# Conv-attention and transformer block on one core: q product in natural order, first attention's matrix work reordered, second-matmul weight splits two steps later

## The reference

```python
# 1. convolutional attention, 1x1 convolutions, softmax along one image axis
q, k, v = (einsum('bchw,oc->bohw', x, w) + b for w, b in ...)   # q, k: 16 channels; v: 128
energy = einsum('bci,bcj->bij', q, k).reshape(b, h, w, h, w)
attn = softmax(energy, axis=-1)
x = gamma * einsum('bchk,bhwkv->bcwv', v, attn) + x
# 2. attention over the 256 tokens of each image, 8 heads of 16, softmax over the n axis
t = tokens(x);  y = layernorm(t)
k, q, v = y @ Wk, y @ Wq, y @ Wv
attn = softmax(einsum('bnhd,bmhd->bnmh', k, q) / 4, axis=n)
t = t + einsum('bnmh,bmhd->bnhd', attn, v)
# 3. mixture of 8 experts, the best 2 per token weighted, 128 -> 512 -> 128
y = layernorm(t);  logits = y @ gate.T;  comb = softmax over the top 2, else 0
for e in range(8):
    out += comb[:, e] * (gelu(y @ w1[e].T + b1[e]) @ w2[e].T + b2[e])
x = t + out
```

## Time and profile before

| | us |
|---|---|
| median of 3 runs | 186.25 (186.21 to 189.31) |
| the profiled execution | 186.13 |
| its span in the trace | 184.2 |
| PE busy | 174.1 (95%) |
| ACT busy | 123.2 (67%) |
| DVE busy | 117.1 (64%) |
| POOL busy | 79.5 (43%) |

### The profile page before, as it was taken

One profiled execution on the slowest core, in us unless ns is written; L12 is line 12 of the kernel. 1 busy time (PEld: TensorE's weight loads), 2 busy tenths in 40 slices (PEclk: granted clock), 3 DMA queues, 4 the chain that ended last, 5 costly groups with the idle time before them and its releaser, 6 DMA issues.

```text
span 184.2 us, 3336 instructions
## 1 busy us (share of the span) xinstructions
PE 174.1 (95%) x1277; PEld 118.6 (64%) x1277; DVE 117.1 (64%) x199; ACT 123.2 (67%) x185; POOL 79.5 (43%) x68
## 2 busy tenths in 40 slices
PE   6999999989898998999999999999999999999991
PEld 3267867665466544447466567567887888888880
DVE  1569544985465396456084959397888677676673
ACT  3516953317727743545988598867878999999970
POOL 8404228988703284452536093524151152333312
PEclk9999999999999999999999999999999999999999
DMA  5799200000000000570000000000000880000001
GB/s 141 276 374 419 96 0 0 4 0 4 0 5 0 2 0 4 181 271 7 0 0 5 0 0 0 4 0 0 0 7 4 244 269 0 0 4 0 0 0 57
DMA packets 5791, 10.94 MB, mean 59 GB/s; under 512 B 1280, under 2 KB 1664, under 8 KB 5520
## 3 DMA queue, kind: packets, MB, share of 16 engines
q1 hardware_dynamic: 5360, 10.65, 16.7%
q10 hardware_dynamic: 416, 0.08, 0.3%
HBM read 10.17 MB, written 0.56 MB: 58 GB/s over the span
## 4 chain that ended last, share of the span: by engine, by line
PE 73%; issue 8%; ACT 7%; POOL 4%; DVE 4%; DMA 2%; ACTq 0%; DVEq 0%; POOLq 0%
PE PS L1159 9%; PE PS L1163 7%; PE PS L1160 7%; PE PS L1186 6%; PE PS L1189 6%; PE PS L1187 6%; PE PS L1181 4%; POOL pairs L357 4%; PE PS L1017 3%; PE PS L1031 3%; ACT room L516 2%; PE PS L910 2%; PE PS L878 2%; PE PS L1104 2%; DMA convw_sb<-convw 2%
## 5 line engine op out<-in xcount | busy, mean ns | idle before, releaser
L516 ACT ACTIVATE room<-PS,b_sb 128x512 f32<-128x512 f32 x64 | 43.6, 688 | 22.6 <-PE PS L1163 21.2
L772 DVE TENSOR_TENSOR Gl<-room,Gh 128x512 fp32r<-128x512 f32 x50 | 41.2, 831 | 13.7 <-ACT Gh L461 13.0
L365 POOL TENSOR_TENSOR x_sb<-x_sb,room 128x512 f32<-128x512 f32 x15 | 23.6, 1572 | 56.0 <-DVE room L781 56.0
L1159 PE MATMUL PS<-x2h,w1h 128*128 128x512 f32 x64 | 27.4, 427 | 1.2 <-ACT room L516 0.8
L461 ACT ACTIVATE Gh<-room 128x512 fp32r<-128x512 f32 x40 | 25.3, 633 | 1.3
L1163 PE MATMUL PS<-x2l,w1h 128*128 128x512 f32 x64 | 25.5, 398 | 0.0
L1160 PE MATMUL PS<-x2h,w1l 128*128 128x512 f32 x64 | 25.2, 393 | 0.0
L1186 PE MATMUL PS<-Gh,w2h 128*128 128x512 f32 x50 | 20.8, 416 | 0.0
L1187 PE MATMUL PS<-Gh,w2l 128*128 128x512 f32 x50 | 19.8, 395 | 0.0
L1189 PE MATMUL PS<-Gl,w2h 128*128 128x512 f32 x50 | 19.7, 395 | 0.0
L1159 PEld LDWEIGHTS PS<-x2h,w1h 128*128 128x128 f32 x64 | 12.0, 187 | 10.6 <-issue 4.9
(11 more groups left out here) (136 smaller groups left out, 294.2 us busy)
## 6 DMA issues: line engine op xcount, KB each, us to landing
room<-comb_rows SPq DMA_DIRECT2D x16, 256.0 KB, 5.2
w1raw<-w SPq DMA_DIRECT2D x8, 256.0 KB, 5.9
w_sb<-w SPq DMA_DIRECT2D x2, 1024.0 KB, 10.6
x_sb<-x SPq DMA_DIRECT2D x2, 256.0 KB, 3.2
dev<-xk SPq DMA_DIRECT2D x1, 512.0 KB, 6.3
out<-x_sb SPq DMA_DIRECT2D x2, 256.0 KB, 4.2
attw_sb<-attw SPq DMA_DIRECT2D x1, 320.0 KB, 6.8
cst<-consts SPq DMA_DIRECT2D x1, 228.5 KB, 6.5
```

The costliest lines, as they stand in the source:

```text
L365: nc.gpsimd.tensor_tensor(t2[:, cols(p)], t2[:, cols(p)], part[:, s, :], ALU.add).then_inc(acc_done, 1)
L516: nc.scalar.activation(G[:, n % GR, :], PS[:, U_BANK[n % 2], :], ACT.Gelu, bias=b1_sb[:, c:c + 1])\
L772: nc.vector.tensor_tensor(Gl[:, n % GR, :], G[:, n % GR, :], Gh[:, n % GR, :].bitcast(f32), ALU.subtract)\
L1159: mm(o, w1h[e][:, ms], x2h[:, cols(p)], start=True, stop=False)
```

## The change

Three edits. The q product of the conv stage takes x in its natural order, and the two copies read PSUM by columns instead. In the first attention the third `project_second` moves ahead of the second raw run, V's projection behind the third raw run and the transposes (whose bank changes from 0 to 1, with the waits adjusted), and `scores(3, s)` stand ahead of `sums(0)` and `sums(1)`. `LOW_W2` shifts `low_weights2` by two steps in POOL's list.

```diff
+        def by_columns(images):
+            return images.rearrange("c (b h w) -> c b w h", b=2, h=H)
...
-        NMT_BANK = [((0, 0), (0, TOK)), ((2, 0), (3, 0))]
+        NMT_BANK = [((1, 0), (1, TOK)), ((2, 0), (3, 0))]
...
-        LOW_W2 = {n + 1: e for n, e in enumerate(W2_ORDER)}
+        LOW_W2 = {n + 3: e for n, e in enumerate(W2_ORDER)}
...
-                nc.scalar.activation(cq[0:C8, pair, :, :, 0].rearrange("c b w h -> c (b w h)"), PS[64:64 + C8, p, :],
+                nc.scalar.activation(cq[0:C8, pair, :, :, 0], by_columns(PS[64:64 + C8, p, :]),
...
-                nc.vector.tensor_scalar(cq[32:32 + C8, pair, :, :, 1].rearrange("c b w h -> c (b w h)"),
-                                        PS[64:64 + C8, p, :], convb_sb[64:64 + C8, 0:1], None, ALU.add)\
+                nc.vector.tensor_scalar(cq[32:32 + C8, pair, :, :, 1], by_columns(PS[64:64 + C8, p, :]), convb_sb[64:64 + C8, 0:1], None, ALU.add)\
...
-                mm(PS[64:64 + C8, p, :].rearrange("c (b w h) -> c b w h", b=2, w=W),
-                   convw_sb[:, 0:C8], x_sb[:, cols(p)].rearrange("c (b h w) -> c b w h", b=2, h=H),
-                   start=True, stop=True)
+                mm(PS[64:64 + C8, p, :], convw_sb[:, 0:C8], x_sb[:, cols(p)], start=True, stop=True)
...
                 if b:
                     pe.wait_ge(prob_ready, 2)
                 else:
-                    pe.wait_ge(v_ready, 2)
+                    pe.wait_ge(act_kq_ready, 6)
...
+                if u == 0 and s == 0:
+                    pe.wait_ge(v_ready, 2)
...
-                if u == 3 and s == 0:
-                    pe.wait_ge(prob_ready, 5)
+                if u == 3:
+                    pe.wait_ge(prob_ready, 4 + s)
...
             project_second(1)
+            project_second(2)
             raw_scores(1)
-            project_second(2)
             project_second(3)
-            project_v(0)
             raw_scores(2)
             image_max_transpose(0)
+            project_v(0)
             raw_scores(3)
...
             values(0)
-            scores(2, 0)
-            scores(2, 1)
+            for u in range(2, 4):
+                for s in range(2):
+                    scores(u, s)
             sums(0)
             sums(1)
-            scores(3, 0)
-            scores(3, 1)
             values(1)
```

## The result

| | before | changed |
|---|---|---|
| median of the runs, us | 186.21 (11 runs) | 188.75 (11 runs) |
| lowest | 186.02 | 187.06 |
| ratio | 1 | 1.0085, 95% interval 1.005 to 1.012 |
| measured again later on another chip | 186.23 | 187.52, ratio 1.0069, interval 1.004 to 1.0099 |

A forecast was written before the change was run, and what follows sets the result against it. PE was taken as the bound, holding 73% of the chain of waits. From 186.13 us, q 0, copies 0, attention +1.1 and gating +0.6 gave 187.8 us; range for 8 in 10: 186.3 to 188.7.

The forecast's parts named there:

- the terms' ends: Bounds given per term: q 1.7 us less, copies 1.1 late, attention 0.8 to 1.5 later, gate's 0.58 wait gone.
- q product: Conv stage: reading x by columns costs PE nothing extra, so natural order gains 0; other end 1.7 us less.
- copies by columns: Conv stage: ACT's and DVE's PSUM copies take no longer, 0; other end 1.1 us late if they double.
- third raw run, from projections: First attention: two projection passes moved ahead of the second raw run let the third start 0.42 us earlier, at 36.19.
- image 1's scores, with V's new place: First attention: V behind the third raw run fits PE's idle time; scores(2, 0) starts 0.3 us earlier, at 44.75.
- end of attention, all in: First attention: pair(2, 0) waits for the delayed sums(0); the end comes 1.1 us later, gain of 0.3 included.
- gate: First expert steps: POOL's back-to-back low parts hold up DVE's small instructions, so PE's step 4 starts 0.6 us later.
- rival 2: Conv stage: by-column reads did cost PE, q passes fall below 0.6 us, total 186.1 us; chance 0.1.
- Rival 1: Gate: DVE's small instructions pass between two low parts, -0.6 instead of +0.6, total 186.6 us; chance 0.25.

The follow-up runs named there:

- second profile: The changed kernel, unedited, profiled in the later measurement on another chip; that measurement's median is 187.52 us.
- scores-only kernel: The kernel before with only scores(3, s) moved ahead of sums(0) and sums(1): 187.46 us, ratio 1.0087.
- the kernel with `sums(0)` between: The changed kernel with sums(0) put between scores(3, 0) and scores(3, 1): 186.11 us, ratio to before 0.9992.
- conv-only kernel: The kernel before with only the conv edit (q product in natural order, copies by columns): 186.09 us, ratio 0.9998.
- the probe: The kernel before with q's first half made twice more behind the second energy quarter, by columns, then in natural order: 188.6 us, one run.
- w2-behind-comb kernel: The kernel before with the w2 splits shifted two steps and POOL waiting for comb before the first: 185.53 us, ratio 0.9966.
- moved-bias kernel: The kernel before with the conv edit and V's bias moved behind the first two energy quarters: 193.65 us, ratio 1.0392.
- the kernel with all gains: The changed kernel with sums(0) between the last scores, POOL waiting for comb, V's bias behind two energy quarters: three runs 184.82 to 185.25 us, four 191.8 to 193.35.

## Why the prediction was right, and where it was not

The median, 188.75, is 1.4% above before and a hair outside my range for 8 in 10, 186.3 to 188.7; the second median, 187.52, lies well inside. By the two comparisons the change costs 0.4 to 1.2%; the forecast was 187.8, 0.9%. That a slowdown came, and from where, was right. My narrower range, 187.3 to 188.4, was called that of the terms' ends, but it holds the attention's ends only, not those that I gave for q, the copies and the gate. The terms, with the second profile:

| term | forecast | measured |
|---|---|---|
| q product | 0 | -0.43 in this profile, nothing in another |
| copies by columns | 0 | 0 (0.70 and 0.75) |
| third raw run, from projections | -0.42 | -0.38 |
| image 1's scores, with V's new place | -0.3 | -0.28 |
| end of attention, all in | +1.1 | +1.10 |
| gate | +0.6 | +0.36 |
| sum | +1.7 | +1.1 |

**The attention** came out step by step. By the second profile, less its 0.43 from the conv stage, the pair starts at 49.0 (forecast 48.9), the third sums at 51.65 (51.55). The wait was found by asking who else waits for the instruction that was moved back: `sums(0)` was never late itself, but it frees a slot of the pairs. The scores-only kernel reproduces it alone, and the kernel with `sums(0)` between gives it back.

**The q product** is the step that failed: "per column both cost the same 1.6 ns", and so "I take the gain as 0". The rows were read rightly and concluded wrongly. In that stretch everything runs at half pace, and at half pace the by-column read costs nothing extra: the first natural-order passes of the conv-only kernel are just as far apart. But the pace doubles at some moment, between 4.4 us and later than 7.9 us in the natural-order profiles, and from there on q's passes follow only in natural order, 0.44 against 0.85 in the probe. Two rows that agree show no price where a third thing bounds both. So the Trainium skill's rule on 16-byte lines ("Advanced Engine Details and Errata", SBUF Cachelines), which I argued away, holds, and rival 2 was right in its mechanism. By its decision point, passes under 0.6 us, it held too. It was wrong in its size, for two reasons: passes that fall into the early half pace gain nothing, and where q is done early, the bias's DMA lands near 7.4 only and the bias then stands in front of the energies, so that of the 1.7 us at most 0.4 arrive. Neither the forecast nor the rival looked at that DMA. That the forecast hardly suffered is luck: the term was small, not nothing.

**The gate** had the right mechanism and a size too large. I had only `g_sum` get through between the first two low parts, and then one instruction per low part. In the trace three small ones pass there (67.01 to 67.5), and `comb` is already the one that waits for the third low part. The next maximum starts at 69.63, which is 68.96 less the lag of 0.67: 0.36 later than before instead of my 0.6. Rival 1 fell: the gap was gone and DVE paid.

**Not forecast at all** was the clock. It makes single executions of any of these kernels 1.3 to 4 us longer, and the first median of the changed kernel lies 1.2 us above the second for no other reason that the runs show. Its executions with a mean clock of 0.995 or more took 187.1 to 188.3, and 12 of 15 were below my 187.8. That the number lies between the two medians is partly luck: my terms were 0.6 too high together, and the clock and the spread of the executions added 0.3 to 1.5.

What stays open is what started the slow stretch in the profile of the changed kernel. PE idled 0.89 us near 7 there; but the conv-only kernel, in whose profile that wait is missing, ran at 0.50 from 14 to 20 us, and the w2-behind-comb kernel, which doesn't have that wait either and in which PE is busy without a gap from 6 to 18 us, shows a mean clock of 0.87 from 9.7 to 23 in its profile as well.

## What to carry to other kernels

When an instruction is moved back in a queue, list what it frees, not only what it makes: here a harmless-looking sum held a buffer slot that a third engine needed. A price read from a stretch in which everything is slow is a price for that stretch only. And before taking "useless" or early work away from in front of a wait, look at PE's clock afterwards: with the bias moved PE idled 1.75 us, the clock fell in 10 of 13 executions, and the time rose by 7 us instead of falling by 1.

## What the runs showed of the hardware

- PE's granted clock fell to 0.50 after 1.75 us without work and stayed there for 16.5 us of unbroken fp32 work (9.5 to 26), in all six executions of the moved-bias kernel by their mean clocks (0.956 to 0.964), and in four of seven of the kernel with all gains. The Trainium skill ("TensorE: Matmul & The Clock Gate", What's actually happening) says that "activity releases the throttle"; in this trace 16.5 us in which PE was never idle did not release it.
- PE's first passes run at half pace, until some moment between 4.4 us and later than 7.9 us, while the granted clock in the profile reads 1.00. The early pace must be read from starts, not from that column.
- A matmul's moving operand in fp32 with a step of 64 bytes: 0.85 us per pass of 512 columns, 0.44 without a step, at a granted clock of 1.00; in the early half pace 0.84 and 0.83, no difference.
- ACT and DVE read PSUM with a step of 64 bytes at no cost: 0.70 and 0.75 us for 16 x 512, against 0.71 to 0.76 and 0.75 before.
- POOL's low parts and DVE's small instructions get in each other's way: beside them the one-hot sum takes 1.06 instead of 0.16 us and `comb` 1.20 instead of 0.19. Between the first two of POOL's low parts three tiny DVE instructions got through (67.01 to 67.5), after that one per low part.
